# Mixer stage of a Mamba-2 and mixture-of-experts block, written anew over six iterations

## Chip, cores and metric

One Trainium2 chip, one core. The metric is the device time of one execution in microseconds. Lower is better.

## What is computed

Two residual sublayers over X of shape (2, 4096, 256) in float32: `x = x + layernorm(mixer(layernorm(x)))`, then `x = x + layernorm(experts(layernorm(x)))`. The change lies in the first and in the router of the second. The mixer:

```python
zxbcdt = jnp.einsum('bld,ed->ble', X, W_in)        # 1288 columns: z 512, x 512, B 128, C 128, dt 8
xBC = silu(conv4(xBC) + conv_b)                    # depthwise, causal, 4 taps, 768 channels
dt = jax.nn.softplus(dt + dt_bias)                 # 8 heads
A = -jnp.exp(A_log)
# per head: h = h * exp(dt*A) + dt*x (outer) B;  y = h . C
y = y + D * x
y = y * silu(z)
y = y * rsqrt(mean(y**2) + eps) * norm_w
out = y @ W_out.T
```

The second sublayer routes each of the 8192 tokens to 8 of 64 experts (capacity 128 each) by softmax and top 8, in order of tokens, and adds a shared expert.

## The kernel before

The kernel has a mixer phase and then an expert phase. The mixer phase goes through the sequence in `STEPS` = 32 steps of 128 tokens of both batches. The five engines each run a list written out by hand, one list for an iteration, inside a loop; semaphores are the only links between them. Iteration `i` holds work of several steps: `j0 = i` (layernorm, projections, convolution, the new decays), `j1 = i - 1` (the scan inside the chunk, the state, gate), `j2` (output projection, second layernorm), `j3`, `j4` (router, top 8, counts). So the order in a list fixes what each engine does next, and an engine stands still when the next entry's semaphore is not there. The first six iterations and the last seven are unrolled; there, entries of steps that don't exist are left out.

The names that matter here:

- `w_in_hi`, `w_in_lo`, `xnt_hi`, `xnt_lo`: the projection runs in fp32r with a high and a low part of both operands, three products for each half of the 256 inputs, so six matmuls for each output group. `xnt_hi` is ScalarE's copy of the transposed layernorm output, `xnt_lo` VectorE's remainder; `xnt_ready` starts the projections.
- The groups of projections: six of conv channels (262 columns moved, L511 to L549), z of batch 0 and of batch 1 (512 columns each, L595 and L585), dt (8 columns for each batch, L524). In z and dt the tokens are the stationary operand and the weights are moved.
- The dt chain on VectorE: `x`, `nabs`, (exp on ScalarE), `w`, `d`, (ln), `num`, `den`, `q`, `inv`, `sp`, `dt`, `a`, `a_grid`, `steps_a`, each 128x16, each waiting for the one before (L876 to L928). It ends in `a_split`, which starts TensorE's sums (L571, L572): three masks times `a` and the mask `upto` times `steps_a`.
- The sums give `decays` (exp on ScalarE, L723) and `run_parts`, which TensorE transposes; ScalarE copies that into `run_fixed` and `run_moving` (L642, L734). `run_fixed` and `run_moving` make the matrices of decays in `bank_s` (L499, L632), whose exp (L655, L680) is multiplied by C B on VectorE (`mix_ready`) and used by TensorE (`intra_done`, L529, L556).
- After these copies ScalarE does the silu's: gate of z (L740, L745), B and C (L743), x (L747).
- On GpSimd: the elementwise work on 128x512 tiles that doesn't read PSUM (L1004): `xw`, the decay of the state, `x_tok` times D, `y` plus that, `y` times the gate, the residual; and the powers for the layernorms.
- PSUM has eight banks; `bank[6]` and `bank[7]` are the two halves of `bank_s`.

VectorE's `eps_o` is L854, `ve_o` a 128x2 entry of L776, `neg_max` L883.

Of the kernel before, what the change touches and what calls it, by code (L numbers as in the profile page):

```python
# [37 lines left out]
KI = DI // P  # L38
EPS = 1e-5
# [24 lines left out]
def build(nc, x_d, w_in_d, conv_w_d, conv_b_d, dt_bias_d, a_log_d, d_d, norm_w_d, w_out_d,  # L64
# [7 lines left out]
    with ctx:  # L72
# [78 lines left out]
        cb = view(NB, P)  # L151
        b_tok = view(NB, NS)
# [42 lines left out]
        steps_a = memory.enter_context(nc.sbuf_tensor("steps_a", [P, NB, 2, NH], F32))  # L195
# [101 lines left out]
        dt_projected = sem("dt_projected")  # L297
# [19 lines left out]
        run_ready = sem("run_ready")  # L317
        projected0, projected1, projected2, projected3, projected4, projected5 = sem("projected0"), sem("projected1"), sem("projected2"), sem("projected3"), sem("projected4"), sem("projected5")
        newest0, newest2 = sem("newest0"), sem("newest2")
        conv_ready0, conv_ready1, conv_ready2 = sem("conv_ready0"), sem("conv_ready1"), sem("conv_ready2")  # L320
        tap0_1, tap0_2, tap1_2 = sem("tap0_1"), sem("tap0_2"), sem("tap1_2")
        bc_ready = sem("bc_ready")
        z_projected0 = sem("z_projected0")
        gate_ready1 = sem("gate_ready1")
        cb_done = sem("cb_done")
        cb_ready = sem("cb_ready")
        b_tok_ready = sem("b_tok_ready")
        x_turned0, x_turned1 = sem("x_turned0"), sem("x_turned1")
        x_tok_ready0, x_tok_ready1 = sem("x_tok_ready0"), sem("x_tok_ready1")
        xdt_ready0, xdt_ready1 = sem("xdt_ready0"), sem("xdt_ready1")  # L330
        xw_ready0, xw_ready1 = sem("xw_ready0"), sem("xw_ready1")
        skip_ready0 = sem("skip_ready0")
# [5 lines left out]
        update_done0, update_done1 = sem("update_done0"), sem("update_done1")  # L338
        state_ready0, state_ready1 = sem("state_ready0"), sem("state_ready1")
        intra_done0, intra_done1 = sem("intra_done0"), sem("intra_done1")  # L340
        y_sum0, y_sum1 = sem("y_sum0"), sem("y_sum1")
        y_ready0, y_ready1 = sem("y_ready0"), sem("y_ready1")
        y_turned0, y_turned1 = sem("y_turned0"), sem("y_turned1")
        squares_ready0, squares_ready1 = sem("squares_ready0"), sem("squares_ready1")
        yt_ready0, yt_ready1 = sem("yt_ready0"), sem("yt_ready1")
        state_decayed1 = sem("state_decayed1")
        skip_added1 = sem("skip_added1")
        out_done1 = sem("out_done1")
        o_stats = sem("o_stats")
# [32 lines left out]
        DEPTH_1, AHEAD = 4, 3  # L382
# [18 lines left out]
        with nc.Block() as block:  # L401
            @block.sync
            def _(eng):
# [13 lines left out]
                def iteration(i):  # L417
                    j0, j3, j4 = i, i - 3, i - 4
                    if real(i + AHEAD):
                        load(i + AHEAD)  # L420
                        eng.wait_ge(x_loaded, 16 * i + (16 * AHEAD + 16))
                        eng.nop(nofuse=True)
                    if real(j3):
# [4 lines left out]
                    if real(j3):  # L428
                        eng.wait_ge(x2t_ready, j3 + 1)
                        eng.nop(nofuse=True)  # L430
                        eng.dma_start(xnt_d[bass.ds(j3, 1), :, :].rearrange("o p f -> (o p) f"), x2t.rearrange("p k b t -> p (k b t)")).then_inc(stored_xnt, 16)
# [12 lines left out]
            def _(eng):  # L444
# [10 lines left out]
                def iteration(i):  # L455
                    j0, j1, j2, j3, j4 = i, i - 1, i - 2, i - 3, i - 4
                    if real(j1):
                        eng.wait_ge(cb_ready, j1 + 1)
                        for b in range(NB):
                            last = transpose(bank[1][:, b * P:(b + 1) * P], xbc[:, 4, b, :])  # L460
                        last
                    if real(j1):
                        if real(j1 - 1):
                            eng.wait_ge(yt_ready0, j1)
                        for c in range(KI):
                            last = transpose(bank[0][:, c * P:(c + 1) * P], xbc[:, c, 1, :])
                        last.then_inc(x_turned1, 1)
                    if real(j1):
                        eng.wait_ge(inter_ready0, j1 + 1)
                        for c in range(KI):  # L470
                            last = transpose(bank[5][:, c * P:(c + 1) * P], xbc[:, c, 0, :])
                        last.then_inc(x_turned0, 1)
                    if real(j2):
                        if real(j2 - 2):
                            eng.wait_ge(logit_ready, j2 - 1)
                        for c in range(KI):
                            last = nc.tensor.matmul(bank[2][:, 0 * DM:1 * DM], yt[:, 0, c, :], w_out[:, c, :], start=c == 0, stop=c == KI - 1)
                        last
                    if real(j2):
                        for c in range(KI):  # L480
                            last = nc.tensor.matmul(bank[2][:, 1 * DM:2 * DM], yt[:, 1, c, :], w_out[:, c, :], start=c == 0, stop=c == KI - 1)
                        last.then_inc(out_done1, 1)
                    if real(j4):
                        eng.wait_ge(chosen_ready, j4 + 1)
                        if real(j4 + 3):
                            eng.wait_ge(x_tok_ready0, j4 + 4)
                        for b in range(NB):
                            last = nc.tensor.matmul(bank[5][b * NE:(b + 1) * NE, 0:P], chosen[:, b, :], upto_bf[:, :], start=True, stop=True)
                        last.then_inc(counts_done, 1)
                    if real(j0):  # L490
                        eng.wait_ge(x_normed, j0 + 1)
                        for b in range(NB):
                            for k in range(KD):
                                last = transpose(bank[0][:, (k * NB + b) * P:(k * NB + b + 1) * P], x_norm[:, b, k * P:(k + 1) * P])
                        last.then_inc(xn_turned, 1)
                    if real(j1):
                        eng.wait_ge(mix_ready1, j1 + 1)
# [6 lines left out]
                    if real(j1):  # L504
                        eng.wait_ge(xw_ready1, j1 + 1)
                        eng.wait_ge(b_tok_ready, j1 + 1)
# [1510 lines left out]
```

## Time and profile before

| | |
|---|---|
| median of 3 runs | 1568.83 us (1557.89 to 2198.08) |
| profiled execution | 1559.98 us, its span 1558.2 us |
| granted TensorE clock, mean of the profiled execution | 0.93 |
| PE busy, share of the span | 1338.7 us, 86% |
| DVE busy | 1098.0 us, 70% |
| ACT busy | 931.3 us, 60% |
| POOL busy | 824.1 us, 53% |

PE is TensorE's matmuls, PEld its weight loads, DVE is VectorE, ACT ScalarE, POOL GpSimd. The mixer phase ends at about 1018 us of the span; the expert phase fills the rest. Shares over the whole span mix the two phases, so the stretch of the mixer is read by itself. A matmul's recorded end is modelled and lies after the start of the next one, so the cost of a matmul in a stream is the distance from one start to the next.

### The profile page before, as it was taken

Reading aid. Unit: us, or ns where it says so; the run is one execution under the profiler, and the core shown is the slowest. Engines: PE = TensorE matmul, PEld = TensorE weight load, DVE = VectorE, ACT = ScalarE, POOL = GpSimd, SP = SyncE. Lnnn points to the kernel's source line nnn. Section 1 sums busy time; section 2 is a strip of 40 time slices with the busy share of each in tenths; the row PEclk is TensorE's granted clock in tenths of the full one; section 3 lists DMA queues with packets and bytes.
Section 4 is the critical chain, followed back from the end, with each engine's and each line's share of the span. In section 5 each row is a group of like instructions: output and inputs, shape, how many; then the busy total and the mean of one; then the engine's idle time right before and its main releaser. Section 6 shows DMA issues by size and latency. Waiting matters only on the chain. (4 is left out here: it accounts for less than half of the span.)

```text
span 1558.2 us, 27694 instructions
## 1 busy us (share of the span) xinstructions
PE 1338.7 (86%) x8642; PEld 1148.7 (74%) x8642; DVE 1098.0 (70%) x3248; ACT 931.3 (60%) x2095; POOL 824.1 (53%) x943
## 2 busy tenths in 40 slices
PE   3899999999999999999999999628887888839995
PEld 3677777778777777777877777528877777739995
DVE  4788888888988888888988888443333333317995
ACT  3766876776776777677677677533333333315664
POOL 0364465456546546545654654426676766633454
PEclk9999999999999999999999999759899989879998
DMA  5400000000000000000000000166666666633443
GB/s 180 142 8 28 31 30 22 29 30 29 29 30 29 29 30 29 22 30 29 29 29 30 23 23 18 39 169 163 155 154 157 159 145 163 154 60 117 141 154 103
DMA packets 110625, 115.64 MB, mean 74 GB/s; under 512 B 19632, under 2 KB 98800, under 8 KB 110576
## 3 DMA queue, kind: packets, MB, share of 16 engines
q1 hardware_dynamic: 95440, 90.38, 18.5%
q0 software_dynamic: 14336, 23.08, 7.9%
q10 hardware_dynamic: 800, 1.57, 0.3%
q8 instruction: 24, 0.39, 0.1%
q14 instruction: 25, 0.20, 0.0%
HBM read 68.53 MB, written 46.47 MB: 74 GB/s over the span
## 5 line engine op out<-in xcount | busy, mean ns | idle before, releaser
L1004 POOL TENSOR_TENSOR mamba_arena<-mamba_arena 128x512 f32<-128x512 f32 (+1 forms) x352 | 383.7, 1107 | 195.3 <-DVE mamba_arena L776 146.6
L1307 PE MATMUL bank<-xt_hi,wsgu_hi 128*128 128x256 f32 x512 | 151.7, 296 | 34.3 <-DVE xt_lo L1759 20.5
L776 DVE TENSOR_TENSOR mamba_arena<-bank,mamba_arena 128x512 f32<-128x512 f32 (+1 forms) x192 | 114.9, 598 | 89.8 <-ACT mamba_arena L751 52.4
L1307 PE MATMUL bank<-xt_lo,wsgu_hi 128*128 128x256 f32 x512 | 146.8, 287 | 0.0
L1307 PE MATMUL bank<-xt_hi,wsgu_lo 128*128 128x256 f32 x512 | 146.7, 287 | 0.0
L446 PE MATMUL bank<-identity,mamba_arena 128*128 128x128 f32 x704 | 102.8, 280 | 31.0 <-ACT mamba_arena L646 31.0
L1307 PEld LDWEIGHTS bank<-xt_hi,wsgu_hi 128*128 128x128 f32 x512 | 100.3, 196 | 36.3 <-DVE xt_lo L1759 21.9
L446 PEld LDWEIGHTS bank<-identity,mamba_arena 128*128 128x128 f32 x704 | 83.1, 146 | 56.6 <-ACT mamba_arena L646 34.4
L776 DVE TENSOR_TENSOR mamba_arena<-mamba_arena 128x512 f32<-128x512 f32 (+2 forms) x192 | 112.4, 588 | 4.4
L1011 POOL TENSOR_SCALAR mamba_arena<-mamba_arena 128x2 f32<-128x2 f32 x32 | 7.1, 221 | 195.5 <-DVE mamba_arena L790 195.5
L642 ACT ACTIVATE mamba_arena<-bank 128x512 f32<-128x512 f32 (+2 forms) x224 | 103.8, 499 | 5.6 <-PE bank L446 4.5
L776 DVE TENSOR_TENSOR mamba_arena<-bank_s,mamba_arena 128x1024 f32<-128x1024 f32 (+1 forms) x96 | 99.8, 1040 | 9.0 <-ACT bank_s L655 7.4
L1307 PEld LDWEIGHTS bank<-xt_lo,wsgu_hi 128*128 128x128 f32 x512 | 100.1, 196 | 0.4
L1307 PEld LDWEIGHTS bank<-xt_hi,wsgu_lo 128*128 128x128 f32 x512 | 100.0, 195 | 0.0
L1314 PE MATMUL bank<-wsdown_hi,act_hi 128*128 128x256 f32 x256 | 78.0, 305 | 0.4 <-DVE act_lo L1741 0.4
L1004 POOL TENSOR_TENSOR mamba_arena<-mamba_arena,minus_half 128x2 f32<-128x2 f32 x96 | 68.1, 709 | 12.4 <-DVE mamba_arena L776 7.1
L646 ACT ACTIVATE mamba_arena<-x_all,mamba_arena 128x256 f32 (+1 forms) x128 | 69.7, 599 | 6.2 <-DVE mamba_arena L816 4.0
L1314 PE MATMUL bank<-wsdown_lo,act_hi 128*128 128x256 f32 x256 | 73.3, 286 | 0.0
L1314 PE MATMUL bank<-wsdown_hi,act_lo 128*128 128x256 f32 x256 | 73.1, 285 | 0.0
L689 ACT ACTIVATE mamba_arena<-mamba_arena 128x16 f32<-128x16 f32 x32 | 6.9, 216 | 106.2 <-DVE mamba_arena L876 106.2
L734 ACT ACTIVATE run_moving<-bank,head_of 64x128 fp32r<-64x128 f32 x256 | 68.3, 361 | 0.4
L529 PE MATMUL bank_s<-mamba_arena 128*128 128x64 f32 x512 | 65.1, 282 | 2.0 <-DVE mamba_arena L776 2.0
(354 smaller groups left out, 4524.9 us busy)
## 6 DMA issues: line engine op xcount, KB each, us to landing
experts_arena<-in_egu SPq DMA_DIRECT2D x64, 256.0 KB, 3.6
routed_sum<-zeros SPq DMA_DIRECT2D x1, 8320.0 KB, 27.0
x_all<-in_x SPq DMA_DIRECT2D x32, 256.0 KB, 2.7
token_table<-mamba_arena SPq DMA_DIRECT2D x64, 128.0 KB, 1.7
normed_transposed<-mamba_arena SPq DMA_DIRECT2D x32, 256.0 KB, 2.0
experts_arena<-normed_transposed SPq DMA_DIRECT2D x32, 256.0 KB, 3.9
experts_arena<-in_edown SPq DMA_DIRECT2D x64, 128.0 KB, 3.3
experts_arena<-routed_sum SPq DMA_DIRECT2D x32, 256.0 KB, 3.4
```

The lines of the kernel that those rows point to most:

```text
L446: return nc.tensor.transpose(out, in_, identity[:, :])
L529: last = nc.tensor.matmul(bank[7][:, h * HD:(h + 1) * HD], decay[:, 1, h, :], xdt[:, 1, h, :], start=True, stop=True)
L642: return nc.scalar.activation(out, in_, ACT.Copy)
L646: last = nc.scalar.activation(out[:, b, :], x[b], ACT.Identity, bias=shift[:, b:b + 1], scale=scale[:, b:b + 1])
L689: nc.scalar.activation(sp["u"], sp["nabs"], ACT.Exp).then_inc(dt_exp, 1)
L734: last = nc.scalar.activation(run_moving[0:HALF, h, :], bank[2][0:HALF, 0:P], ACT.Copy, scale=head_of[0:HALF, h:h + 1])
L776: return nc.vector.tensor_tensor(out, a, b, op)
L1004: return nc.gpsimd.tensor_tensor(out, a, b, op)
L1011: nc.gpsimd.tensor_scalar(ve_x, mv_x[:, :, 1], EPS, None, ALU.add).then_inc(x_var, 1)
L1307: last = nc.tensor.matmul(out[:, f * 256:(f + 1) * 256], w[:, k, columns], x[:, k, :], start=n == 0, stop=n == len(parts) - 1)
L1314: last = nc.tensor.matmul(out[:, b * DM:(b + 1) * DM], x[:, c, b * P:(b + 1) * P], w[:, c, :], start=c + n == 0, stop=c == FS // P - 1 and ...
```

## The change

All engine lists of the mixer loop are written in a new order, spread over `j0` to `j5` (`DEPTH_1` from 4 to 5, so one more iteration; seven and eight iterations are unrolled). Within that:

- The columns of `W_in` are laid out anew on the host: 248 of z, the 8 of dt, the other 264 of z, then x, B and C. One group of matmuls of 256 columns for each batch gives the first 248 of z and dt (into the two halves of `bank[1]`); one group of 264 columns for each batch gives the rest of z (`bank[0]`, `bank[6]`). The separate dt group is gone.
- `steps_a` and `a` lie side by side in `a_all`, so one matmul with `upto` does both.
- B in token layout (`b_tok`) is transposed in the same iteration as C B, into the same bank, and one ScalarE copy takes both (`cb_b`).
- The transposes of x to token layout (`x_tok`) and `xdt[0]` move from the next iteration into the same one, behind ScalarE's silu's.
- `eps_o`, `ve_o` and `neg_max` go from VectorE to GpSimd.
- The store of `x2t`, the logits and the copy of the logits move from `j3` to `j4`.
- Most entries are in another order and use other banks, so most waits are new.

The core of the diff (of the new order, TensorE's projections, sums and the end of its list, ScalarE's end, GpSimd's list):

```diff
+ZA = DI // 2 - NH
-        cb = view(NB, P)
-        b_tok = view(NB, NS)
+        cb_b = view(2, NB, P)
+        cb, b_tok = cb_b[:, 0], cb_b[:, 1]
-        steps_a = memory.enter_context(nc.sbuf_tensor("steps_a", [P, NB, 2, NH], F32))
+        a_all = memory.enter_context(nc.sbuf_tensor("a_all", [P, 6 * NH], F32))
+        steps_a = a_all[:, 0:4 * NH].rearrange("p (b k h) -> p b k h", b=NB, k=2)
+        sp["a"] = a_all[:, 4 * NH:6 * NH].rearrange("p (b h) -> p b h", b=NB)
-        DEPTH_1, AHEAD = 4, 3
+        DEPTH_1, AHEAD = 5, 3
 # TensorE
-                        for b in range(NB):
-                            for n, k, x, w in terms(xnt, w_in):
-                                last = nc.tensor.matmul(bank[1][:, b * NH:(b + 1) * NH], x[:, k, b, HALO:], w[:, k, DI + CONV:], start=n == 0, stop=n == LAST)
-                        last.then_inc(dt_projected, 1)
+                        for b in range(NB):
+                            for n, k, x, w in terms(xnt, w_in):
+                                last = nc.tensor.matmul(bank[1][:, b * (ZA + NH):(b + 1) * (ZA + NH)], x[:, k, b, HALO:], w[:, k, 0:ZA + NH], start=n == 0, stop=n == LAST)
+                        last.then_inc(z_projected0, 1)
...
+                        eng.wait_ge(a_split, j0 + 1)
+                        nc.tensor.matmul(bank[4][:, 0:6 * NH], upto[:, :], a_all[:, :], start=True, stop=True)
+                        for q, mask in enumerate((beyond, ones)):
+                            last = nc.tensor.matmul(bank[4][:, (q + 3) * NB * NH:(q + 4) * NB * NH], mask[:, :], a_all[:, 4 * NH:6 * NH], start=True, stop=True)
+                        last.then_inc(sums_done, 1)
...
+                        eng.wait_ge(xc_ready, j0 + 1)
+                        eng.wait_ge(conv_ready2, j0 + 1)
+                        for c in range(KI):
+                            last = transpose(bank[7][:, c * P:(c + 1) * P], xbc[:, c, 0, :])
+                        last.then_inc(x_turned0, 1)
...
+                        eng.wait_ge(bc_ready, j0 + 1)
+                        for b in range(NB):
+                            nc.tensor.matmul(bank[3][:, b * P:(b + 1) * P], xbc[:, 4, b, :], xbc[:, 5, b, :], start=True, stop=True)
+                        for b in range(NB):
+                            last = transpose(bank[3][:, (NB + b) * P:(NB + b + 1) * P], xbc[:, 4, b, :])
+                        last.then_inc(cb_done, 1)
 # ScalarE, behind the table load
+                        eng.wait_ge(z_projected1, j0 + 1)
+                        nc.scalar.activation(gate_z[:, 0, ZA:DI], bank[0][:, 0:DI - ZA], ACT.Silu).then_inc(gate_ready1, 1)
...
+                        nc.scalar.activation(gate_z[:, :, 0:ZA], bank[1][:, :].rearrange("p (b f) -> p b f", b=NB)[:, :, 0:ZA], ACT.Silu).then_inc(gate_ready0, 1)
+                        eng.wait_ge(conv_ready1, j0 + 1)
+                        nc.scalar.activation(xbc[:, 0:KI], half[:, 0:KI], ACT.Silu).then_inc(xc_ready, 1)
```

The new lists of the loop, in order (the step in brackets, `<-` a wait on another engine):

- TensorE: update of state 0 (j1), out 1 (j2), logits (j4) `<- x2t_ready`, transposes of `x_norm` (j0) `<- x_normed`, intra 0 (j1) `<- mix_ready0`, decay matrix 1 (j1), projections 1 `<- xnt_ready`, 0, z and dt first part, 3, 2, 4, 5 (j0), transposes of y 0 (j1) `<- conv_ready0`, intra 1 (j1), sums (j0) `<- a_split`, z second part 0, transpose of `run_parts` `<- run_split`, update of state 1 (j1), out 0 (j1), transposes of y 1 (j1), z second part 1 (j0), counts (j4), transposes of x 0 `<- xc_ready, conv_ready2`, of x 1, C B and B (j0) `<- bc_ready`, decay matrix 0 (j0), read of state 0 (j0), transposes of `x2_norm` (j3) `<- cb_ready`, read of state 1 (j0).
- ScalarE: table, exp of matrix 0 (j1), `x2t` (j4), `x_norm` (j0), `xnt_hi`, `x2_norm` (j3), logits (j4), exp of matrix 1 (j1), `half` 1, 0, squares 0, exp for dt `<- dt_nabs`, `half` 3, ln for dt `<- dt_more`, `half` 2, 4, 5, `yt` 0, `o_norm` (j2), `expd` (j4), `decays` `<- sums_done`, table, gate, copies of run, gate, silu of x `<- conv_ready1`, silu of B and C `<- conv_ready2`, gate, `x_tok` 0 and 1, `cb_b` `<- cb_done`, `yt` 1, squares 1, tanh.
- VectorE: statistics of x, `xdt[1]` (j1), `count_now` (j5), `y` 0 and 1 from the state (j1), mix 0 (j1), statistics of out (j2), `xnt_lo` (j0), `y_sum0` `<- intra_done0`, top 8 (j4), state 0 (j1), mix 1 (j1), taps of `half` 0 and 1 with `shift_o`, `chosen`, dt's `x`, `nabs`, `w` between them, `d` to `a_split`, taps of `half` 2 and 3 with `y_sum1` and `run_parts` between them, taps of `half` 4 and 5, state 1, `top_sum`, `xdt[0]` (j0), statistics of x2 (j2), counts (j4).
- GpSimd: powers for x (j0) and x2 (j3), `x_tok[0]` times D, `y` 0 plus that, decay of state 0, `y` 0 times gate `<- y_sum0`, `eps_o`, `ve_o`, power (j2), `x_tok[1]` times D, decay of state 1, `y` 1 plus, halo casts `<- projected5`, `xw[1]`, `neg_max` (j4), `y` 1 times gate `<- y_sum1`, residual (j2), `picked`, `weights` (j4), `xw[0]` (j0) `<- xdt_ready0`.

## Rows read from the trace of the kernel before

**Rows 1.** windows: length, then busy PE, PEld, DVE, ACT, POOL, clock.
```profile
402.01:431.81 29.80, 27.65 (x175) 22.17 (x174) 26.30 (x74) 21.90 (x50) 16.23 (x20) 1.00 0.09 29
...
20.20:942.50 922.30, 861.97 (x5233) 699.24 (x5234) 794.96 (x2212) 666.47 (x1480) 481.75 (x592) 0.97 0.11 36
942.50:1018.60 76.10, 57.19 (x305) 45.55 (x304) 48.22 (x158) 48.38 (x96) 37.00 (x48) 0.82 0.09 32
1018.60:1558.20 539.60, 419.57 (x3106) 403.92 (x3106) 247.20 (x860) 211.45 (x516) 303.68 (x292) 0.88 0.56 144
```

**Rows 2.** waits of 400 to 700 us: total us, times, longest.
```profile
PE bank L571 <- DVE steps_a L928: 5.9, 6, 1.0
...
PE bank L534 <- DVE mamba_arena L776: 5.7, 10, 0.6
```

**Rows 3.** timeline of PE, one iteration: start, us, engine, line, op, tiles.
```profile
404.86 1.89 PE L477 MATMUL bank<-mamba_arena 128*128 128x256 f32 x8
406.59 1.89 PE L481 MATMUL bank<-mamba_arena 128*128 128x256 f32 x8
...
412.91 0.25 PE L524 MATMUL bank<-w_in_hi,xnt_lo 128*128 128x8 f32 x1
...
413.91 0.25 PE L524 MATMUL bank<-w_in_hi,xnt_lo 128*128 128x8 f32 x1
...
419.10 0.28 PE L549 MATMUL bank<-xnt_lo,w_in_hi 128*128 128x262 f32 x1
419.22 0.28 PE L549 MATMUL bank<-xnt_hi,w_in_hi 128*128 128x262 f32 x1
...
419.67 2.00 PE L556 MATMUL bank<-mamba_arena 128*128 128x64 f32 x16
421.51 0.61 PE L446 MATMUL bank_s<-identity,mamba_arena 128*128 128x128 f32 x4
423.09 0.39 PE L571 MATMUL bank<-mamba_arena,upto 128*128 128x16 f32 x2 [0.98 <-DVE steps_a L928]
...
424.00 0.63 PE L446 MATMUL bank<-identity,mamba_arena 128*128 128x128 f32 x4
...
424.94 0.40 PE L585 MATMUL bank_s<-w_in_hi,xnt_lo 128*128 128x512 f32 x1
425.18 0.40 PE L585 MATMUL bank_s<-w_in_hi,xnt_hi 128*128 128x512 f32 x1
```

**Rows 4.** DVE groups by form, 400 to 700 us: busy us, mean ns.
```profile
L776 DVE TENSOR_TENSOR mamba_arena<-mamba_arena 128x2 f32<-128x2 f32 x10 | 11.5, 1152 | 0.3
...
L854 DVE TENSOR_SCALAR mamba_arena<-mamba_arena 128x2 f32<-128x2 f32 x10 | 10.0, 1002 | 0.0
L883 DVE TENSOR_SCALAR mamba_arena<-mamba_arena 128x2 f32<-128x2 f32 x10 | 9.5, 950 | 0.0
```

**Rows 5.** timeline of DVE, the same iteration.
```profile
414.50 1.15 DVE L776 TENSOR_TENSOR mamba_arena<-mamba_arena 128x2 f32<-128x2 f32 x1
...
420.49 1.14 DVE L776 TENSOR_TENSOR mamba_arena<-mamba_arena 128x16 f32<-128x16 f32 x1
```

**Rows 6.** timeline of POOL, the same iteration.
```profile
414.37 1.26 POOL L1004 TENSOR_TENSOR mamba_arena<-mamba_arena 128x512 f32<-128x512 f32 x1
...
419.88 0.20 POOL L1047 CAST xnt_hi<-xnt_hi 128x12 fp32r<-128x12 f32 x1 [1.35 <-PE bank L549]
```

**Rows 7.** timeline of DVE in the drain, POOL idle.
```profile
1001.39 0.16 DVE L776 TENSOR_TENSOR mamba_arena<-mamba_arena 128x2 f32<-128x2 f32 x1
```

**Rows 8.** timeline of ACT, the same iteration.
```profile
424.27 0.21 ACT L723 ACTIVATE mamba_arena<-bank 128x48 f32<-128x48 f32 x1 [0.99 <-PE bank L572]
...
425.29 1.28 ACT L727 ACT_TABLE_LOAD   x1
...
429.16 0.61 ACT L740 ACTIVATE mamba_arena<-bank 128x512 f32<-128x512 f32 x1
...
430.63 1.08 ACT L747 ACTIVATE mamba_arena<-mamba_arena 128x1024 f32<-128x1024 f32 x1
```

More of the change, by code:

```diff
@@ L468, in iteration @@
[L468 to L478, printed above, removed]
@@ L479, in iteration @@
-                    if real(j2):
-                        for c in range(KI):
-                            last = nc.tensor.matmul(bank[2][:, 1 * DM:2 * DM], yt[:, 1, c, :], w_out[:, c, :], start=c == 0, stop=c == KI - 1)
+                        if is_number(j1) and real(j1):
+                            eng.wait_ge(cb_ready, j1 + 1)
+                        eng.wait_ge(xw_ready0, j1 + 1)
+                        if real(j1 - 4):
+                            eng.wait_ge(counts_ready, j1 - 3)
+                        nc.tensor.matmul(bank[1][:, :], b_tok[:, 0, :], flat(xw[:, 0]), start=True, stop=True)
@@ L490, in iteration @@
+                        last.then_inc(logits_done, 1)
                     if real(j0):
@@ new lines, in iteration @@
+                        for h in range(NH):
+                            last = nc.tensor.matmul(bank[5][:, h * HD:(h + 1) * HD], decay[:, 0, h, :], xdt[:, 0, h, :], start=True, stop=True)
+                        last.then_inc(intra_done0, 1)
+                    if real(j1):
+                        for q in range(2):
+                            nc.tensor.matmul(bank_s[:, q, :], run_fixed[:, 1, :], run_moving[:, 4 * q:4 * q + 4, :].rearrange("p h t -> p (h t)"),
+                                             start=True, stop=False)
+                            last = nc.tensor.matmul(bank_s[:, q, :], identity_bf[:, :], later_bf[:, :].unsqueeze(1).broadcast_to([P, 4, P]),
+                                                    start=False, stop=True)
+                        last.then_inc(seg_done1, 1)
@@ new lines, in iteration @@
+                    if real(j1):
+                        if is_number(j1) and real(j1):
+                            eng.wait_ge(mix_ready1, j1 + 1)
+                        for h in range(NH):
+                            last = nc.tensor.matmul(bank[2][:, h * HD:(h + 1) * HD], decay[:, 1, h, :], xdt[:, 1, h, :], start=True, stop=True)
+                        last.then_inc(intra_done1, 1)
+                    if real(j0):
+                        if real(j0 - 1):
+                            eng.wait_ge(yt_ready0, j0)
+                        eng.wait_ge(a_split, j0 + 1)
[3 more added lines that the diff above has]
+                        last.then_inc(sums_done, 1)
@@ new lines, in iteration @@
+                    if real(j4):
+                        if is_number(j4) and real(j4):
+                            eng.wait_ge(chosen_ready, j4 + 1)
+                        if real(j4 + 4):
+                            eng.wait_ge(gate_ready0, j4 + 5)
+                        for b in range(NB):
+                            last = nc.tensor.matmul(bank[1][b * NE:(b + 1) * NE, 0:P], chosen[:, b, :], upto_bf[:, :], start=True, stop=True)
+                        last.then_inc(counts_done, 1)
@@ L552, in iteration @@
-                    if real(j1):
-                        if real(j1 + 1):
-                            eng.wait_ge(conv_ready0, j1 + 2)
-                        for h in range(NH):
-                            last = nc.tensor.matmul(bank[5][:, h * HD:(h + 1) * HD], decay[:, 0, h, :], xdt[:, 0, h, :], start=True, stop=True)
-                        last.then_inc(intra_done0, 1)
+                        nc.tensor.matmul(bank[4][:, :], xbc[:, 5, 0, :], flat(state[:, 0]), start=True, stop=True).then_inc(read_done0, 1)
@@ L627, in iteration @@
[L627 to L636 removed]
+                        nc.tensor.matmul(bank[5][:, :], xbc[:, 5, 1, :], flat(state[:, 1]), start=True, stop=True).then_inc(read_done1, 1)
```

680 lines of the change are left out of this document (333 added, 347 removed).

## The prediction

> **What bounds the kernel now.** I read the windows first [rows 1]. The mixer loop takes 922.3 us from the first step's start to the last one's, 31 periods of 29.75; a steady iteration is 29.80. Its drain takes 76.1 and the expert phase 539.6, and the change touches nothing of the latter. In a steady iteration TensorE is busy for 27.65 of 29.80 at a granted clock of 1.00 (its 2.4 GHz level), VectorE 26.30, ScalarE 21.90, GpSimd 16.23. So TensorE is nearly the bound and VectorE is close behind, and both must become shorter for a real gain. Next I read who TensorE waits for [rows 2]: VectorE alone, at two chains above all, the end of dt's chain (`steps_a`, about 1 us where it occurs) and the addition that frees a bank (0.6). All waits make 29.80 - 27.65 = 2.15 us an iteration. Last the timeline of one iteration, for the distances between starts [rows 3] and for what the small VectorE operations really cost [rows 4 to 7].
>
> **TensorE's work.** dt's matmuls move 8 columns but start 0.111 us apart (412.91 to 413.91 are nine steps) [rows 3]; twelve go: -1.33 us. z before: 12 of 512 columns at 0.235 = 2.82. After: 12 of 256 and 12 of 264 columns. No row shows these with tokens stationary; the nearest is 262 columns, 0.12 apart, and half a 512 gives 0.117, so 2.81 to 2.90, and I take 2.88 (+0.06) [rows 3]. The sums: four fp32 matmuls take 424.00 - 423.09 = 0.91, so one fewer is -0.23 and three cost 0.68 [rows 3]. The transposes of B, the logits and the rest are moved, not changed. In all -1.5 us an iteration.
>
> The Trainium skill (TensorE: Matmul & The Clock Gate, section Back-to-back issue gap) puts a warm matmul at its columns over 2.4 GHz and 2.5 ns, with a floor of about 25 ns. An estimate by that alone gives 0.3 us for dt's twelve and a net gain of 0.4 instead of 1.5. The trace differs: 0.111 us for 8 columns. The same page's section LDWEIGHTS has 107 ns for 128 columns of weights, which fits the row; so the gap's figure doesn't decide here.
>
> **VectorE's work.** `eps_o` (1.00), `ve_o` (1.15) and `neg_max` (0.95) leave: 3.1 us [rows 4]. They are dear only by where they stand: `ve_o` starts at 414.50, lasts 1.15 and ends at 415.65, and a GpSimd operation that started at 414.37 ends at 415.63; `q` of the dt chain loses about as much [rows 5, 6]. With GpSimd idle the same entry takes 0.16 [rows 7]. So a small operation with its operands in SBUF waits until the running GpSimd operation is through, and the taps that read PSUM don't. Own work afterwards: 26.3 - 3.1 = 23.2, with about 1 us of `q`'s wait still in it.
>
> **GpSimd's work.** Three entries more, 0.2 each by the halo cast and at most 0.4 with their wait [rows 6]: +0.6 to 1.2, on an engine that is busy for 16 of 30 us. Behind them in the queue stands the power for `o_scale`, needed by ScalarE much later. I take 0.9, hidden; uncovered it would stand in full.
>
> **ScalarE's work.** C B and B in one copy instead of two; the gate in three pieces instead of two; no row shows these shapes, and I bound each by a saving or a loss of 0.3, together nothing. The other edits that move a store, the logits or `x2t` to `j4` issue the same DMAs, one entry later on SyncE's queue, and nothing waits for them within an iteration.
>
> **The loop that closes.** The new lists decide which waits meet. Walk from TensorE's transposes of x, at the end of an iteration, to the same in the next:
>
> 1. TensorE's full stretch, through the reads, state 0, out 1, logits, intra 0, one decay matrix and all projections but z's second part. Work after: 27.65 - 1.5, less about 0.7 of tails of the matmuls that stand before a wait = 25.5. Outside the stretch lie out 0 (1.73), intra 1 (1.84), sums (0.68), z's second parts (1.45), update of state 1 (0.86, half of out's), eight transposes of y (0.9), run and counts (0.3) = 7.8 [rows 3]. So 17.5 to 17.7; I take 17.5. Inside it every input comes in time: the chain from the statistics of x over GpSimd, ScalarE, transposes, `xnt_lo` is ready a microsecond or more before the decay matrix ends, because the x transposes and C B now follow in TensorE's queue.
> 2. GpSimd: at the end of the last projection the halo casts (0.35 with their latency), `xw[1]` (1.05 to 1.26) and `neg_max` (0.2) = 1.8 [rows 6]. They stand in the way because dt's chain is under way then: `nabs` and the exp come after the taps and after `chosen`, which have each lost a turn to the run of GpSimd operations in front, so `w` and `d` are due just as `xw[1]` starts.
> 3. VectorE from `d` to `a_split`: `q`'s start 420.49 to the sums' 423.09 is 2.6, less the 1.0 that `q` lost, plus three steps of 0.16 = 2.1 [rows 3, 5, 7]. GpSimd is idle in that time, since its next entry waits for `y_sum1`, which is behind the chain.
> 4. Sums 0.7 and 0.2 of latency, `decays` 0.21, table load 1.28, a gate piece 0.3, the copies of run 2.59 (426.57 to 429.16), gate 0.5, silu of x 1.08, and the x transposes start [rows 8]: 6.8.
>
> Together 17.5 + 1.8 + 2.1 + 6.8 = 28.2 us. A second path of about the same length runs inside it: the taps of `half` 0 and 1 also end late by these lost turns (near 18.5 to 19 on this scale), then y's transposes 0.45 and intra 1 1.84 give 21.2, and the sums start at 21.4. So TensorE idles about as much as before, in other places: before y's transposes, before the sums, before x's transposes. The gain is what its work lost.
>
> 31 periods x (29.75 - 28.2) = 48 us. Fill and drain: one iteration more, but its added part holds a copy of one column; `x_tok` is made earlier and the logits later, so I take 0, with 5 us to either side. 1559.98 - 48 = 1512 us. The profiled execution lies 0.6% under the median of the three runs, and the sum is made against it.
>
> **Rivals.**
>
> A. GpSimd and VectorE don't meet. If dt's chain gets through before `xw[1]`, step 2 and the lost turns fall away, and TensorE's own work is the bound: 25.5 plus tails and one or two unavoidable waits = 26.2 to 27. For it: VectorE's own work of 23 leaves room. Against it: `nabs`, exp, `w`, ln, `d` are five links over two engines, and GpSimd has three 128x512 operations in front without a wait. At 26.6: 1559.98 - 31 x 3.15 = 1462.
>
> B. One more turn or a late ScalarE. `w` and `xw[1]` come within 0.2 us of each other in my walk; if `w` loses, the taps and so y's transposes and intra 1 move by 1.1 and the period is 29.2; the same comes of a table load or copies that start 1 us later, for before, the transposes of x were not behind the silu's. 1559.98 - 31 x 0.55 = 1543.
>
> C. Slower: the bound becomes VectorE with its lost turns. In an iteration it has some 16 operations with two operands in SBUF or of the kind of `eps_o`: dt's chain, `xdt`, shifts, `chosen`. GpSimd has ten 128x512 operations, which now run in other places. 23.2 + 8 x 1.0 = 31.2, so 1559.98 + 31 x 1.45 = 1605. It decides from the seventh lost turn on (29.8 - 23.2 = 6.6); my walk has three or four. For it: each turn does cost 1 us [rows 4]. Against it: the chain's long end lies in GpSimd's wait for `y_sum1`. The Trainium skill (SBUF — State Buffer, section Who interferes with whom) states the lock itself: a VectorE instruction with two SBUF inputs or in a two-port mode and a GpSimd one exclude each other for the whole instruction, whoever is first. The trace agrees for `eps_o` and `ve_o` (1.00 and 1.15 against 0.16).
>
> That the change doesn't do what it says I don't hold possible for the work: the dt group is gone from the list. It can be for the gain, which is B.
>
> **How the numbers follow.** The forecast with periods of 27.6 to 28.7 (1493 to 1527) has a chance of 0.62, A 0.14, B 0.17, C 0.07. The time is the likeliest's, 1512. The range leaves out most of C and the far half of A and B: 1464 to 1550, which takes in the fill (5 us), 0.3 of ScalarE (9 us) and the bounds of the stretch and of `xw[1]` (0.2 each, 12 us). Within 2% means 1529 to 1591, about what a measurement of this kernel can tell from no change: faster 0.75, same 0.19, slower 0.06.
>
> **What would show it.** An iteration of 28.2 in the windows, TensorE busy near 26.3 of it. No 8-column matmuls; z's pieces 0.12 apart. VectorE's `nabs`, `w`, `d` or `chosen` at about 1 us where GpSimd runs, and the rest of the chain at 0.17. TensorE waiting for VectorE before y's transposes and before the sums, and for ScalarE's silu before the transposes of x. ScalarE's table load right behind `decays`. The prediction is wrong if `xw[1]` doesn't meet the chain (A), if TensorE waits for `mix_ready` or for `xnt_ready` (then the stretch isn't full, and the walk's first step fails), or if fill and drain grow by more than 5 us.

## The result and the profile after

The changed kernel takes 1493.68 us (median of 4 runs, 1492.71 to 1494.59), the kernel before 1564.03 (4 runs; one of them took 2198.08 us and doesn't enter the ratio). The ratio is 0.9559, with a 95% interval from 0.9528 to 0.959: faster by 4.4%. The profiled execution took 1492.71 us, its span 1491.0. The forecast was 1512.

The windows of the kernel after, with the same columns as [rows 1]: one steady iteration, the loop from the first step's start to the last one's, the drain, the rest.

```profile
399.80:427.68 27.88, 25.86 (x173) 21.38 (x172) 24.96 (x72) 22.14 (x50) 16.91 (x24) 1.00 0.09 31
20.70:881.20 860.50, 788.80 (x5172) 651.53 (x5173) 754.91 (x2127) 670.15 (x1480) 502.42 (x678) 1.00 0.12 39
881.20:955.00 73.80, 52.36 (x302) 41.42 (x300) 44.86 (x146) 50.80 (x99) 38.80 (x58) 0.81 0.11 37
955.00:1491.00 536.00, 418.31 (x3106) 402.77 (x3106) 247.47 (x860) 211.51 (x516) 302.36 (x291) 0.89 0.57 144
```

Against [rows 1]: the loop gave 61.8 us, 922.3 to 860.5. The drain with the boundary to the expert phase gave about 5 more, the expert phase about 1. In a steady iteration TensorE's busy time went from 27.65 to 25.86, but its idle time hardly moved, 2.15 to 2.02. The clock column of the loop went from 0.97 to 1.00; this turned out to matter.

The waits of TensorE in that iteration (us in total, times, longest) answer to [rows 2]:

```profile
PE bank L449 <- DVE mamba_arena L900: 0.9, 1, 0.9
PE bank_s L449 <- ACT mamba_arena L762: 0.7, 1, 0.7
PE bank L564 <- DVE a_all L931: 0.4, 1, 0.4
```

Before y's transposes, before x's transposes, before the sums. These are the three places that the prediction named. TensorE's timeline has them, and between them the terms of the walk:

```profile
403.51 0.66 PE L449 MATMUL bank_s<-identity,mamba_arena 128*128 128x128 f32 x4 [0.70 <-ACT mamba_arena L762]
...
417.00 0.28 PE L520 MATMUL bank<-w_in_hi,xnt_hi 128*128 128x256 f32 x1
417.12 0.29 PE L520 MATMUL bank<-w_in_lo,xnt_hi 128*128 128x256 f32 x1
...
420.51 0.28 PE L541 MATMUL bank_s<-xnt_lo,w_in_hi 128*128 128x262 f32 x1
421.65 0.66 PE L449 MATMUL bank<-identity,mamba_arena 128*128 128x128 f32 x4 [0.86 <-DVE mamba_arena L900]
...
424.44 0.39 PE L564 MATMUL bank<-a_all,upto 128*128 128x48 f32 x2 [0.40 <-DVE a_all L931]
```

VectorE's and GpSimd's timelines of the same stretch are read side by side:

```profile
418.75 0.82 DVE L887 SCALAR_TENSOR_TENSOR mamba_arena<-mamba_arena 128x16 f32<-128x16 f32 x1
...
420.27 0.55 DVE L895 TENSOR_SCALAR mamba_arena<-mamba_arena 128x16 f32<-128x16 f32 x1
...
421.52 0.78 DVE L904 TENSOR_SCALAR mamba_arena<-mamba_arena 128x16 f32<-128x16 f32 x1
...
423.91 0.17 DVE L928 TENSOR_SCALAR a_all<-mamba_arena 128x16 f32<-128x16 f32 x1
```

```profile
414.76 1.30 POOL L1012 TENSOR_TENSOR mamba_arena<-mamba_arena 128x512 f32<-128x512 f32 x1 [0.72 <-DVE mamba_arena L791]
416.15 0.19 POOL L1046 TENSOR_SCALAR mamba_arena<-mamba_arena 128x2 f32<-128x2 f32 x1
...
416.70 0.70 POOL L1012 TENSOR_TENSOR mamba_arena<-mamba_arena,minus_half 128x2 f32<-128x2 f32 x1
417.36 3.42 POOL L1012 TENSOR_TENSOR mamba_arena<-mamba_arena 128x512 f32<-128x512 f32 x3
420.93 0.20 POOL L1065 CAST xnt_hi<-xnt_hi 128x12 fp32r<-128x12 f32 x1
421.07 0.20 POOL L1066 CAST xnt_lo<-xnt_lo 128x12 fp32r<-128x12 f32 x1
421.22 1.04 POOL L1012 TENSOR_TENSOR mamba_arena<-mamba_arena 128x512 f32<-128x512 f32 x1
```

`nabs` (L887), `w` (L895) and `d` (L904) take 0.55 to 0.82 beside GpSimd's run of three operations and beside `xw[1]` (421.22); once GpSimd is still, a link of the same size takes 0.17. `eps_o` on GpSimd (416.15) takes 0.19.

### The profile page after: what moved, and what is told of

The parts are those of the page before. It is cut to its first block and busy times, and to the rows that moved or that the text cites. A ratio compares the mean times of both kernels' runs of the same rounds, so it can differ in the third digit from the quotient of the medians.

```text
span 1491.0 us, 27525 instructions
## 1 busy us (share of the span) xinstructions
PE 1259.5 (84%) x8578; PEld 1095.7 (73%) x8578; DVE 1054.9 (71%) x3152; ACT 937.5 (63%) x2097; POOL 845.2 (57%) x1039
## 5 line engine op out<-in xcount | busy, mean ns | idle before, releaser
L1012 POOL TENSOR_TENSOR mamba_arena<-mamba_arena 128x512 f32<-128x512 f32 (+2 forms) x384 | 383.3, 1009 | 298.9 <-DVE mamba_arena L791 201.3
L449 PE MATMUL bank<-identity,mamba_arena 128*128 128x128 f32 x704 | 112.2, 279 | 53.4 <-DVE mamba_arena L900 27.2
L791 DVE TENSOR_TENSOR mamba_arena<-bank,mamba_arena 128x512 f32<-128x512 f32 (+1 forms) x224 | 136.3, 610 | 14.6 <-PE bank L493 7.8
L657 ACT ACTIVATE mamba_arena<-bank 128x512 f32<-128x512 f32 x192 | 100.3, 539 | 6.6 <-PE bank L449 3.8
L791 DVE TENSOR_TENSOR mamba_arena<-mamba_arena 128x512 f32<-128x512 f32 (+1 forms) x128 | 54.7, 427 | 48.9 <-ACT mamba_arena L657 46.7
L791 DVE TENSOR_TENSOR mamba_arena<-bank_s,mamba_arena 128x1024 f32<-128x1024 f32 x64 | 77.8, 1216 | 2.4 <-ACT bank_s L696 2.2
L589 PEld LDWEIGHTS bank<-mamba_arena 128*128 128x128 f32 x256 | 46.9, 192 | 31.1 <-ACT mamba_arena L747 17.8
L589 PE MATMUL bank<-mamba_arena 128*128 128x256 f32 x256 | 64.4, 395 | 0.6
L471 PEld LDWEIGHTS bank<-mamba_arena 128*128 128x128 f32 x256 | 48.5, 190 | 20.0 <-issue 14.9
```

Of the source, the lines that this page charges most:

```text
L449: return nc.tensor.transpose(out, in_, identity[:, :])
L471: last = nc.tensor.matmul(bank[0][:, 1 * DM:2 * DM], yt[:, 1, c, :], w_out[:, c, :], start=c == 0, stop=c == KI - 1)
L589: last = nc.tensor.matmul(bank[0][:, 0 * DM:1 * DM], yt[:, 0, c, :], w_out[:, c, :], start=c == 0, stop=c == KI - 1)
L657: return nc.scalar.activation(out, in_, ACT.Copy)
L791: return nc.vector.tensor_tensor(out, a, b, op)
L1012: return nc.gpsimd.tensor_tensor(out, a, b, op)
```

## The experiments

Each kernel ran once with a profile unless said otherwise. The kernel before, run beside them on the same chip, took 1564.15, 1561.61 and 1559.6 us in the three sets; eleven later runs of it spread from 1556.27 to 1568.67, so totals of single executions that differ by a few us say little. Therefore I set the mean clock of each of the 31 periods (from one step's start to the next one's) beside its length. Of the 29 periods behind the fill, those at a clock of 1.00 agree within 0.1 us or so in the middle of the loop, so their median measures a schedule far better than one total time does:

| kernel | us | period at clock 1.00 | periods with a lower clock, their mean |
|---|---|---|---|
| before (profiled) | 1559.98 | 29.81 | 17, 30.04 |
| `before_dt_cut` | 1556.59 | 29.81 | 15, 29.92 |
| `before_small` | 1539.08 | 28.99 | 19, 29.47 |
| `before_both` | 1552.97 | 29.00 | 22, 30.17 |
| `before_both_fill` | 1536.84 | 29.02 | 1, 29.02 |
| after (profiled) | 1492.71 | 27.89 | 0 |
| `dt_apart` | 1500.7 | 28.01 | 1, 28.54 |
| `small_on_dve` | 1506.44 | 28.23 | 3, 29.98 |
| `silu_first` | 1492.84 | 27.80 | 0 |
| `gpsimd_order` | 1480.07 | 27.52 | 1, 29.48 |
| `both_orders` | 1479.94 | 27.46 | 3, 28.97 |
| `run_cut` | 1458.8 | 26.72 | 0 |
| `gpsimd_cut` | 1436.68 | 26.23 | 0 |

**dt's group apart again, in the new order.**

```diff
-  matmul(bank[1][:, b * (ZA + NH):(b + 1) * (ZA + NH)], x[:, k, b, HALO:], w[:, k, 0:ZA + NH], ...)
+  matmul(bank[1][:, b * (ZA + NH):b * (ZA + NH) + ZA], x[:, k, b, HALO:], w[:, k, 0:ZA], ...)
+  # and behind both batches, as a group of its own:
+  matmul(bank[1][:, b * (ZA + NH) + ZA:(b + 1) * (ZA + NH)], x[:, k, b, HALO:], w[:, k, ZA:ZA + NH], ...)
```

> The changed kernel with dt's eight columns as a group of their own again (248 columns and 8 columns for each batch), in the same place. Theory (TensorE's work lies on the loop that closes): twelve matmuls more at 0.111 us each in the full stretch, so a period of 29.2 instead of 27.88 and 1491 + 31 x 1.3 = 1531 to 1535 us. Rival (VectorE's relief made the gain, and TensorE's saved work only turned into idle time): the period stays within 0.3 of 27.88, at most 1503 us.

1500.7 us. Windows of one iteration, then TensorE's waits in it:

```profile
408.66:436.67 28.01, 26.93 (x185) 22.66 (x184) 24.60 (x71) 22.34 (x50) 16.87 (x23) 1.00 0.09 31
```

```profile
PE bank_s L449 <- ACT mamba_arena L765: 0.7, 1, 0.7
PE bank L567 <- DVE a_all L934: 0.3, 1, 0.3
```

Twelve matmuls more and 1.07 us more work, but a period only 0.12 longer: the wait of 0.9 before y's transposes is gone. My theory, which gave TensorE's work its full price, missed by 30 us; both numbers are inside the rival's.

**The small sums back on VectorE, in the new order.**

```diff
 # GpSimd's list
-  nc.gpsimd.tensor_scalar(eps_o, ...); tt(ve_o, mv_o[:, :, 1], eps_o, ALU.add); nc.gpsimd.tensor_scalar(neg_max, ...)
 # VectorE's list: behind mv_o's aggregates, and neg_max behind the second taps of half 0 and 1
+  nc.vector.tensor_scalar(eps_o, ...); tt(ve_o, mv_o[:, :, 1], eps_o, ALU.add); nc.vector.tensor_scalar(neg_max, ...)
 # not shown: three semaphore waits of ScalarE and GpSimd that the move makes necessary inside the loop
```

> The changed kernel with eps_o, ve_o and neg_max on VectorE again: the first two behind the statistics of the output, neg_max behind the second taps. Theory (a lost turn costs only where it is on the loop): eps_o and ve_o meet one GpSimd operation and delay y_sum0 by about 0.7, neg_max delays the taps by up to 0.8 and leaves GpSimd's queue ahead of the chain; period 28.4 to 28.9, 1507 to 1523 us. Rival (VectorE is the bound): all three at about 1 us as in the kernel before, period near 30.9, 1585 us.

1506.44 us, 28.23 a period: 0.34 longer at full clock, and three periods near 30.0 at 0.89. The way was right and the rival is far off, but both numbers lie just under the theory's ranges: I had priced the lost turns on the loop too high.

**GpSimd's operations of batch 1 cut to two columns.**

```diff
-  tt(x_tok[:, 1], x_tok[:, 1], per_head(d_skip), ALU.mult)
+  tt(flat(x_tok[:, 1])[:, 0:2], flat(x_tok[:, 1])[:, 0:2], d_skip[:, 0:2], ALU.mult)
 # the same for the decay of state[:, 1], y[:, 1] plus x_tok[:, 1], and xw[:, 1]; state 1's update reads xdt
```

> The changed kernel with four GpSimd operations of batch 1 cut to two columns (x_tok times D, decay of the state, y plus that, xw), and the update of the state reading xdt instead of xw; so the D term, the decay of the state and the weights of batch 1 are left out. Theory (dt's chain meets these operations on the loop): small VectorE steps at 0.17, no wait before y's transposes, TensorE's own work the next bound; period 26.3 to 26.6, 1443 to 1452 us. Rival (lost turns are hidden): period 27.5 or more, 1479 us or more.

1436.68 us, 26.23 a period, both just under the theory's ranges.

```profile
411.96:438.16 26.20, 25.47 (x173) 21.26 (x172) 23.14 (x71) 22.22 (x50) 13.11 (x23) 1.00 0.09 33
```

VectorE has the same instructions as after, yet is busy for 1.8 us less, 23.14 against 24.96: these are its lost turns. TensorE waits once, 0.7 for the silu of x. The cut could also have helped by making GpSimd's results come earlier, but in both kernels the only wait of another engine for GpSimd is one of 0.3 on VectorE (L820), and it is unchanged. So 1.66 us of 27.89 are meetings with GpSimd.

**Only the run of three cut, `xw[1]` whole.** The edit is the first three of the four above.

> The changed kernel with three GpSimd operations of batch 1 cut to two columns (x_tok times D, state decay, y plus), the run between the power and the halo casts; xw[1] stays whole. It leaves out the D term and the state's decay in batch 1. The cut of all four took the period from 27.88 to 26.22. If xw[1] meeting dt's chain is the dear meeting, as the prediction's second step says, 0.6 us or less go here: period 27.3 or more, 1473 or above. If the run in front is (the chain's exp and taps late by its lost turns), 1.0 to 1.7 go: 26.2 to 26.9, 1436 to 1462.

1458.8 us, 26.72 a period, inside the range given for the run in front. That run is worth 1.17, and `xw[1]` another 0.49 once the run is gone. VectorE's timeline has `nabs`, `w` and `d` at 0.16 to 0.17 now, but a later link of dt's chain meets `xw[1]` (404.96 to 406.00):

```profile
405.10 0.93 DVE L919 SCALAR_TENSOR_TENSOR mamba_arena<-mamba_arena 128x16 f32<-128x16 f32 x1
```

**ScalarE's silu of x ahead of its second gate piece.**

```diff
 # ScalarE
+  activation(xbc[:, 0:KI], half[:, 0:KI], ACT.Silu)
   activation(gate_z[:, :, 0:ZA], ...)
-  activation(xbc[:, 0:KI], half[:, 0:KI], ACT.Silu)
 # TensorE: the counts (which need that gate) go from ahead of x's transposes to behind them
```

> The changed kernel with ScalarE's silu of x ahead of the gate of 496 columns, and TensorE's counts behind the transposes of x. Theory (the loop closes through ScalarE's tail): the transposes of x start 0.48 earlier, period 27.4, 1476 to 1479 us. Rival (VectorE's list is the bound, ScalarE's tail hidden): no change, 1490 to 1493 us.

1492.84 us, 27.80 a period: a miss. The transposes of x start 6.49 behind the sums instead of 6.96. But from them to decay matrix 0 it is 1.89 instead of 1.52. The counts, which stood in TensorE's wait before, are now inside that stretch (0.17); the other 0.2 is in the spacing around C B, where the profile shows no wait of TensorE, and what causes it stays open.

**dt's work cut in the kernel before.**

```diff
-  for n, k, x, w in terms(xnt, w_in):
-      matmul(bank[1][:, b * NH:(b + 1) * NH], ..., start=n == 0, stop=n == LAST)
+  for n, k, x, w in terms(xnt, w_in)[:1]:
+      matmul(bank[1][:, b * NH:(b + 1) * NH], ..., start=True, stop=True)
```

> The kernel before with eleven of dt's twelve 8-column matmuls taken out for each step (ten, in fact, with one kept for each batch: two of twelve stay). It leaves out most terms of dt's projection; the number of every other instruction is the same. This is what the change takes from TensorE, but in the old order and with the small sums where they were. If the gain is what TensorE's work lost (the prediction's sentence), 10 x 0.111 = 1.1 us an iteration go: 31 x 1.1 = 34 us, near 1530. If the engines lie side by side and TensorE's work only fills its waits (what the group of its own showed in the new order: 0.26 an iteration), 0.2 to 0.5 an iteration: 1549 to 1558.

1556.59 us beside 1561.61, and at full clock 29.81, the same as before to the hundredth. The total lies in the range of the second theory, but the period says less than its 0.2 to 0.5: nothing at all. Waits of this kernel from 400 to 700 us, ten iterations:

```profile
PE bank L534 <- DVE mamba_arena L776: 11.3, 10, 1.1
PE bank L571 <- DVE steps_a L928: 4.9, 5, 1.0
PE bank_s L529 <- DVE mamba_arena L776: 4.0, 10, 0.4
```

Against [rows 2] the wait of projection 3 for VectorE (L534; it is VectorE's read of dt that frees the bank) doubled, from 5.7 to 11.3, and one of 0.4 an iteration in front of intra 1 (L529) is new, while the one before the sums fell from 5.9 to 4.9. That makes 0.9 us an iteration more of waiting, where I had reckoned with 1.1 less of work.

**The small sums on GpSimd in the kernel before.** The mirror of the second edit: `eps_o` and `ve_o` ahead of the power for `o_scale`, `neg_max` behind the halo casts.

> The kernel before with eps_o, ve_o and neg_max on GpSimd instead of VectorE and the waits that this needs written out. If VectorE's lost turns are what the loop pays for, this brings 0.4 to 1.0 us an iteration, 1533 to 1552 (undoing it in the new order cost 0.44). If TensorE's work alone binds, nothing: 1560 to 1566.

1539.08 us, within the theory's range; 28.99 at full clock, so 0.82 a period. At the lower clock the periods were 29.47 on average.

**Both in the kernel before.**

> Both edits in the kernel before: two of dt's twelve matmuls stay (the others are left out) and the small sums on GpSimd. Theory (the new order of the lists made most of the 1.99 us an iteration): no more than 1.0 us an iteration together, 1533 or above. Rival (the two reliefs made the gain, the order nothing): 1.6 us an iteration or more, 1514 or below.

1552.97 us. That is in the theory's range (1533 or above), but the two reliefs together are worse than the small sums alone by 14 us, which neither theory had. At full clock the period is 29.00, as with the small sums alone; but 22 of 29 periods are not at full clock. Windows of two neighbouring periods and of the stretch in the second where the clock is down:

```profile
398.92:427.91 28.99, 26.29 (x165) 21.00 (x165) 25.49 (x72) 22.04 (x49) 16.84 (x23) 1.00 0.09 28
427.91:458.09 30.18, 27.79 (x165) 22.35 (x165) 25.61 (x73) 22.04 (x49) 16.85 (x23) 0.94 0.09 30
446.70:450.10 3.40, 3.40 (x13) 3.02 (x14) 3.33 (x10) 1.99 (x3) 1.70 (x3) 0.52 0.07 28
```

The same 165 matmuls take 1.5 us longer. TensorE's timeline has the place:

```profile
443.78 0.61 PE L447 MATMUL bank_s<-identity,mamba_arena 128*128 128x128 f32 x4
446.08 0.40 PE L572 MATMUL bank<-mamba_arena,upto 128*128 128x16 f32 x2 [1.69 <-DVE steps_a L921]
...
448.50 0.63 PE L586 MATMUL bank_s<-w_in_lo,xnt_hi 128*128 128x512 f32 x1
448.92 0.63 PE L586 MATMUL bank_s<-w_in_hi,xnt_lo 128*128 128x512 f32 x1
...
450.79 0.40 PE L596 MATMUL bank<-w_in_lo,xnt_hi 128*128 128x512 f32 x1
```

TensorE waits 1.69 us for dt's chain before the sums, and z's matmuls behind start 0.42 apart, where they start 0.24 apart at full clock [rows 3].

**The gap filled.** To the kernel with both reliefs, more work for TensorE:

```diff
-  for b in range(NB):
+  for b in [0, 1] * 4:
       for k in range(KD):
           last = transpose(bank[7][:, (k * NB + b) * P:(k * NB + b + 1) * P], x2_norm[:, b, k * P:(k + 1) * P])
```

> The kernel before with both reliefs (two of dt's twelve matmuls left, small sums on GpSimd) and twelve more transposes ahead of the sums: the four of x2's normalised rows are made four times, 12 x 0.11 = 1.3 us of work for TensorE where it otherwise waits 1.7 us for dt's chain. Theory (the clock): the reliefs leave TensorE idle in one piece there, the granted clock falls to 0.50 behind it, and that costs 0.9 to 2.1 us in each period in which it happens; with the gap filled the clock stays at 1.00, nearly all periods take 28.99, and the time comes down to 1528 to 1540 although TensorE has more work. Rival (the long periods have another cause): the extra work changes nothing or costs up to 1.3 us a period, 1553 to 1590.

1536.84 us. Twelve more matmuls an iteration brought 16 us against `before_both`, one execution of each; it is about the time of the small sums alone (1539.08). The waits from 400 to 700 us now have the sums at 0.4, and the loop's row has a clock of 1.00:

```profile
PE bank L572 <- DVE steps_a L921: 4.3, 11, 0.4
```

```profile
20.57:913.48 892.91, 837.31 (x5259) 675.28 (x5260) 771.20 (x2126) 668.29 (x1480) 500.01 (x677) 1.00 0.11 38
```

28 of 29 periods are at full clock, 29.02 long. So the clock made `before_both` slow, and not the order in which its waits end: at full clock its period is the same with and without the extra work.

**GpSimd's order, in the new kernel.** GpSimd waits before it multiplies `y` 0 by the gate (414.76 above), and then has its run in dt's chain. The state's decay can go ahead of that wait, and `xw[1]` ahead of the halo casts:

```diff
+  eng.wait_ge(read_done1, j1 + 1)
+  tt(state[:, 1], state[:, 1], per_head(decays[:, 2, 1, :]), ALU.mult)
   eng.wait_ge(y_sum0, j1 + 1)
   tt(flat(y[:, 0]), flat(y[:, 0]), gate_z[:, 0, :], ALU.mult)
   ...
-  tt(state[:, 1], state[:, 1], per_head(decays[:, 2, 1, :]), ALU.mult)
   ...
+  tt(xw[:, 1], xdt[:, 1], per_head(decays[:, 1, 1, :]), ALU.mult)
   # the halo casts
-  tt(xw[:, 1], xdt[:, 1], per_head(decays[:, 1, 1, :]), ALU.mult)
```

> The changed kernel with two GpSimd operations moved: the decay of state 1 goes ahead of y0's gate, where GpSimd waits 3.2 us for VectorE, and xw[1] goes ahead of the halo casts, where it waits for TensorE. The work is the same. If GpSimd's run of 128x512 operations after that wait is what makes dt's chain lose its turns late, the run ends 1 us sooner and up to 0.35 us an iteration go (the small reliefs overlap): 1483 to 1491. If TensorE's stretch is the later end anyway, 1492 to 1495; if state decay now meets VectorE's decay matrices and shifts, up to 1500.

1480.07 us, under the range; 27.52 a period, 0.37 less, where the first theory allowed 0.35 at most. (The wait before y0's gate is 0.72 us; the 3.2 of the expectation belong to y1's gate.) GpSimd's timeline:

```profile
466.29 3.42 POOL L1012 TENSOR_TENSOR mamba_arena<-mamba_arena 128x512 f32<-128x512 f32 x3
469.66 0.19 POOL L1068 CAST xnt_hi<-xnt_hi 128x12 fp32r<-128x12 f32 x1
```

`xw[1]` is now the third of the run, and the casts follow it at once. `d` takes 0.16 (0.78 after), and from the last projection's end (about 469.3) to `d`'s end (470.6) it is 1.3 instead of 1.65: this is where the 0.37 came from. TensorE no longer waits before the sums. Its wait before y's transposes grew from 0.9 to 1.1, and the sums follow intra 1 at once (472.80). So the second path, which the prediction put just behind the chain, has become the later one; a still shorter chain alone would not start the sums earlier.

**With the silu's order as well.** Both edits together.

> The changed kernel with GpSimd's two operations moved and, on ScalarE, the silu of x ahead of the second gate piece with TensorE's counts behind x's transposes. Periods of full clock were 27.52 with the first edit and 27.80 with the second against 27.88. If they add, 27.4: 1476 to 1479. If the second edit's wait for the silu of B and C decides again, 27.5: 1479 to 1483.

1479.94 us, 27.46 a period. They nearly add at full clock (27.43 if they did), but three periods fell to a lower clock, and the total is the same.

**`gpsimd_order` timed in five rounds.**

> The kernel with GpSimd's two operations moved again, timed in turns with the kernel before. One look gave 1480.07 beside 1561.61. From that, 1477 to 1483 and a ratio of 0.945 to 0.950 to the kernel before; the changed kernel stood at 0.9559 with an interval from 0.9528 to 0.959, so a ratio under 0.9528 says that this version beats both. If the look was a lucky execution (no period with a fallen clock), it comes at 1485 to 1494.

1483.77 us (median of 6, 1480.29 to 1493.37) beside 1560.76 (11 runs). The ratio to the kernel before is 0.9504, interval 0.947 to 0.9539. The median lies between the two expectations (up to 1483, or from 1485). It beats the kernel before clearly. Against the changed kernel (0.9559, from 0.9528) the median is 10 us lower, but the intervals overlap a little and the ratio isn't under 0.9528 with its whole interval, so I call it probably better. Its spread is wider, and the clock goes with it: the fastest run has a mean granted clock of 0.944, the slowest, 1493.37 us, of 0.935. In the profiled one two periods fell to a lower clock, 29.14 and 29.48 us against 27.53.

## Why the prediction came out as it did

**The walk's sum was right, its first term 0.4 too long.** From x's transposes (403.51) to the last projection's end (about 420.6) is 17.1 where I had 17.5. The other terms measured 1.65 (1.8; from the last projection to the end of `d`), 2.15 (2.1) and 6.96 (6.8). Together 27.9 against 28.2. That the stretch of the first term has no wait inside held. TensorE's busy time is 25.86, where the prediction's sum gave 26.15 and its list of signs 26.3. Over 31 periods, which average 27.76, this is 14 of the 19 us by which the profiled execution beat the forecast; the drain is 5, which I had put at "0, with 5 us to either side".

**The step that failed is "So TensorE idles about as much as before, in other places ... The gain is what its work lost".** The idle time did stay, 2.15 to 2.02, but that is a coincidence and no cause: with dt's group apart again it is 28.01 - 26.93 = 1.08. Taking most of dt's work away in the old order gave 0.00 us a period at full clock; putting it all back in the new order cost 0.12. TensorE was never the bound by itself: its waits stretch or shrink by what its work changes.

**What makes the gain.** The loop's 61.8 us split so: 29 periods x (29.81 - 27.89) = 55.7; the 17 periods before at a lower clock, 17 x (30.04 - 29.81) = 3.9; the fill's two periods 2.4. Of the 1.92 us a period, the small sums alone give 0.82 in the old order. With dt's work cut as well it is 0.81 (`before_both`). What remains, 1.1, is put down to the new lists together with the single matmul for `a_all` and the single copy for C B and B by subtraction alone; no run has them by themselves, so how they share it stays open. The split also depends on the order in which it is made: in the new order the small sums are worth only 0.34, since other ends have moved close, and everything else then 1.58.

**GpSimd's part held, VectorE's only without the meetings.** The three entries take 0.19 to 0.25 on GpSimd, and its busy time grew by 0.7 as forecast (0.6 to 1.2). VectorE's own work of 23.2 is near the 23.14 of `gpsimd_cut`, but in the changed kernel it is busy for 24.96: the turns that it loses in the new order stand in the walk and not in that sum. The Trainium skill (SBUF — State Buffer, section Who interferes with whom) has a VectorE instruction with two SBUF inputs and a GpSimd one that reads SBUF exclude each other for the whole instruction. The trace agrees for `nabs`, whose two inputs are both `x` in SBUF: 0.82 beside the run, 0.24 in `dt_apart`, where it started at 420.90 and GpSimd's operation ended at about 421.1, and 0.17 in `run_cut`, where GpSimd was idle.

**Step 2 named one meeting of two.** I put only the meeting at `xw[1]` on the path as a price. Moving it away, together with the state's decay, gave 0.37, and `d` then lost no turn, so it is there (the two moves were not made one by one); but the run of three in front of the halo casts is the dear one, 1.17. It delays `nabs`, so the exp, `w` and the taps. It is not what makes the chain meet `xw[1]`: without the run the chain meets it too, at L919. And `chosen`, which the walk had losing a turn, lost none (0.28 beside the run, 0.29 without it).

**Rival A's price was right, and its condition isn't met.** With all four operations cut, and so no meetings in dt's chain, the period is 26.23, at the low end of A's 26.2 to 27; with `xw[1]` whole it is 26.72. In the changed kernel the engines do meet. B and C didn't come: five small operations of VectorE lose time to GpSimd (`nabs`, `w`, `d`, L837 and L878, 0.46 to 0.82 each instead of about 0.16), together about 2.6 us, where C needed 6.6.

**What no part of the prediction looked at is the clock.** I read 1.00 in the steady iteration and left it; the loop's own row in [rows 1] says 0.97. In the kernel before it cost little in the middle of the loop, because TensorE had slack behind it: the waits of a period at full clock (404.12 to 433.93) and of one at 0.94 (463.84 to 493.75) differ by the one before the sums, which the slow stretch has used up.

```profile
PE bank L571 <- DVE steps_a L928: 1.0, 1, 1.0
PE bank L534 <- DVE mamba_arena L776: 0.6, 1, 0.6
PE bank L595 <- DVE mamba_arena L955: 0.4, 1, 0.4
```

```profile
PE bank L534 <- DVE mamba_arena L776: 0.6, 1, 0.6
PE bank L595 <- DVE mamba_arena L955: 0.4, 1, 0.4
```

In `before_both` it decided the total.

## What to carry to other kernels

Where three engines end side by side, price an edit by the walk from wait to wait, and check it in both orders: one undone in the new kernel and one done in the old. Two operations on GpSimd moved ahead of its own waits were worth 0.37 us a period, three times as much as twelve matmuls less on TensorE (0.12). Compare periods at the same granted clock before you compare totals, and if relief on TensorE makes a kernel slower, look for one long wait in front of the slow stretch.

## What the runs showed of the hardware

- The granted clock fell to its lower level (1.2 GHz) behind single waits of TensorE: for 3.4 us in `before_both` behind one of 1.69 (446.7 to 450.1, above), and for 6.8 us in `before_small` (443.2 to 450.0) behind one of 1.13. With no slack behind it a period took 0.3 to 2.1 us longer (`before_both`, 29.25 to 31.14 against 29.00), with slack 0.1 in the middle of the loop (before, 29.90 against 29.81). The Trainium skill (TensorE: Matmul & The Clock Gate, section A second HAM failure mode: psum-queue depth-cycling) describes a kernel in which small idle pieces of TensorE between groups of matmuls make the clock swing between its two levels. The traces agree as far as the clock swung here too, though no wait of TensorE from 400 to 700 us in `before`, `before_small` or `before_both` was longer than 1.7 us.
- Not every such wait brings it down: `before_both` has the wait of 1.7 us in each of ten iterations, and the clock fell in most periods, not in all. What decides stays open. In the kernel before it fell in the middle of a wait of only 0.57 (at about 475.9):

```profile
474.24 1.39 PE L529 MATMUL bank_s<-mamba_arena 128*128 128x64 f32 x11
476.20 0.59 PE L534 MATMUL bank<-xnt_hi,w_in_hi 128*128 128x262 f32 x1 [0.57 <-DVE mamba_arena L776]
...
477.02 0.42 PE L534 MATMUL bank<-xnt_hi,w_in_hi 128*128 128x262 f32 x1
477.24 0.42 PE L534 MATMUL bank<-xnt_hi,w_in_lo 128*128 128x262 f32 x1
```

  The wait need not be the cause there. Ahead of it stand dt's twelve matmuls of 8 columns and sixteen of 64 columns, and the same stretch with the same wait in the period from 404.12 brought no fall. With ten of the twelve left out (`before_dt_cut`, where that wait is 1.1) still 15 periods have a lower clock.
- Extra matmuls in such a wait kept the clock up in `before_both_fill`: one period below full clock instead of 22, and 16 us less than `before_both`.
